# Attention stage of a two-layer kernel: key scores on 32 rows in pairs, projections and halves moved, a norm moved to ScalarE

## The chip, the cores and the metric

The program runs on one core of a Trainium2 chip. The metric is the device time of one execution in microseconds (us), lower is better. A run gives the median of several executions; one further execution was taken with the hardware profiler.

## The reference

Two layers over x of shape 4 x 512 x 128 (2048 tokens of 128 features). The change touches layer 0's attention and the layer norm and routing behind it. Cut to that:

```python
def _L0_attn_ref(x, WQ, WK, WV, WO):            # 16 heads of 8, causal
    Q, K, V = (heads(WQ), heads(WK), heads(WV))
    score = jnp.einsum('bhqd,bhkd->bhqk', Q, K) / jnp.sqrt(jnp.asarray(D_K, x.dtype))
    score = score + mask
    score = score - jnp.max(score, axis=-1, keepdims=True)
    score = jnp.exp(score)
    score = score / jnp.sum(score, axis=-1, keepdims=True)
    out = jnp.einsum('bhqk,bhkd->bhqd', score, V)
    out = out.transpose(0, 2, 1, 3).reshape(B, S, E)
    return out @ WO

x = L0_attn_x
x = x + _L0_attn_ref(_layernorm(x, axis=-1), WQ, WK, WV, WO)
x = x + _L0_ffn_ref(_layernorm(x, axis=-1), ...)   # 8 experts, top 2, fixed capacity
x = x + _L1_attn_ref(_layernorm(x, axis=-1), ...)  # gated linear attention + feed-forward
x = x + _L1_ffn_ref(_layernorm(x, axis=-1), ...)
```

## The kernel before

The program has three parts: layer 0's attention (up to about 214 us of the span), the eight experts, and layer 1. Only the first is changed.

**How attention is tiled.** There are 4 batches b of 512 tokens and 4 groups g of 4 heads, so 16 steps w = 4 b + g. Queries and keys are split into a rounded half and a rest and laid out as planes: a head takes 32 partitions (8 features in 3 or 4 planes, so that products of fp32r numbers come out near fp32). QS and QM are 128 x 512, four heads of 32 partitions. KP[:, s, j, i, :] is 128 x 128 for key tile j and head i, and holds numbers only on the 32 partitions of head i; the rest is zero. In a step these things are made:

- **row scores** of the step after (`row_scores`, line 1615): 10 units of 128 queries by 4 x 128 keys, 4 of them with a mask product (line 1618). VectorE takes the row maximum of each (`row_max`, line 1052) and frees the bank. They go round 3 PSUM banks (0 to 2), in the order that `_ring` gives, together with the two projections of the next batch.
- **turn_max** (line 1657): the maxima are transposed into bank 7, and `add_max` (line 1066, VectorE) adds them to QS, which gives QM.
- **key scores** (`key_scores`, line 1631): 12 units n, 4 heads for each of 3 chunks of key tiles: units 0 to 3 have one product of 512 columns, 4 to 7 one of 384, 8 to 11 two, of 256 and 128. They go round 3 more banks (3 to 5). Unit n waits for the exponential of unit n-3, which ScalarE makes (`exp_unit`, line 679). Units 10 and 11 are issued in the step after.
- **values** (`values`, line 1643): for key tile j, 4 heads, each with 32 output columns of the array and an fp32 moving operand (the trace gives their shape as 128*32, rows by columns of the array; all other matmuls are 128*128). They wait for `select` on GpSimd. values(w, 0) comes in step w, values 1 to 3 in step w+1.
- **turn_out** (line 1665) and `normalise` (VectorE) for the step before.

**Once a batch.** In the steps with g = 0, `project` (lines 1602, 1603) makes Q and K of the next batch, `round_halves` (line 669, ScalarE) rounds them to HL, `make_halves` (line 1042, VectorE) makes the rests and frees the two banks, and SyncE stores the planes to HBM and later loads them as QS and KP (`store_planes`, `pad`, lines 390 to 416). SyncE's KP of step G waits, from G = 3 on, for the key scores of step G-3. In the same steps `turn_heads` (line 1671) transposes the finished heads of the batch before, in g = 1 they are multiplied by WO (line 1677), VectorE adds them to X (line 1088) and makes the statistics of a layer norm (`stats_`, lines 957 to 963), GpSimd raises variances to -0.5 (`rsqrt`, line 521), and VectorE applies it (`norm`, line 969); in g = 2 the result is transposed (`turn_normed`) and gives the router's logits, in g = 3 the ranks.

**What sets the order.** Every engine's program is written out by hand in a loop over w; there is no scheduler. Semaphores tie the engines. Each engine runs its instructions in the order written.

Of the kernel before, what the change touches and what calls it, by code (L numbers as in the profile page):

```python
# [56 lines left out]
def _ring():  # L57

    at = {("q", 0): 0, ("k", 0): 1}
    for G in range(NW):  # L60
        for u in range(10):
            at[u, G] = len(at)
        if G % NG == 1 and G // NG + 1 < NB:
            at["q", G // NG + 1] = len(at)
            at["k", G // NG + 1] = len(at)
    return at
# [42 lines left out]
def build(nc, d):  # L109
    ctx = ExitStack()  # L110
    with ctx:
# [95 lines left out]
        with ExitStack() as attention:  # L207
# [15 lines left out]
            VR = early("VR", [P, NT, P])  # L223

# [85 lines left out]
        varA, rsA, xnA = sem("varA"), sem("rsA"), sem("xnA")  # L310
# [179 lines left out]
        def _(g):  # L490
# [58 lines left out]
            for w in range(NW):  # L549
# [4 lines left out]
                if at == 1 and before >= 0:  # L554
                    rsqrt(varA, rsA, before + 1)
# [86 lines left out]
        def _(act):  # L642
# [50 lines left out]

            def take_turn(what, b, dst):
# [42 lines left out]
            for w in range(NW):  # L737
# [4 lines left out]
                exp_unit(w, 0)  # L742
                if b and g == 2:
                    take_turn("turn2", b - 1, xn2T[:, :])
                exp_unit(w, 1)
# [7 lines left out]
                exp_unit(w, 5)  # L753
                exp_unit(w, 6)
                exp_unit(w, 7)
                if g == 0 and b + 1 < NB:
                    round_halves(b + 1)
                exp_unit(w, 8)
                if b and g == 0:
                    take_turn("turn", b - 1, OT[:, :])  # L760
                exp_unit(w, 9)
            exp_unit(NW - 1, 10)
# [171 lines left out]
        def _(v):  # L934
# [144 lines left out]
            def tail_of(b):  # L1079
# [9 lines left out]
                def stats_():  # L1089
                    v.wait_ge(tp_free, TURNS["wo", b] + 1)  # L1090
                    ln_stats(xt, link, varA)

                def norm():

                    v.wait_ge(scattered, b * 16 * TOPK * TB)
                    ln_apply(xt, lambda t: xn[:, t, :], rsA, b + 1, xnA)
# [55 lines left out]
                return add, stats_, norm, take_logits, choose, spread, ranks, place, count  # L1152
# [5 lines left out]
            for w in range(NW):  # L1158
                b, g = w // NG, w % NG
                rows_next = w + 1 < NW  # L1160
                if b and g == 0:
                    add, stats_, norm, take_logits, choose, spread, ranks, place, count = tail_of(b - 1)
                if rows_next:
# [404 lines left out]
        def _(pe):  # L1568
# [53 lines left out]
            def key_scores(w, n):  # L1622
# [555 lines left out]
```

## Time and profile before

| | us |
|---|---|
| median of 3 runs | 658.8 (657.65, 658.8, 662.22) |
| the profiled execution | 656.35, its span 654.6 |
| TensorE busy | 583.0 (89% of the span) |
| VectorE busy | 402.2 (61%) |
| ScalarE busy | 316.2 (48%) |
| GpSimd busy | 172.9 (26%) |
| mean granted TensorE clock | 0.965 |

Times in the trace are from the first instruction. PE is TensorE's matmuls, PEld its weight loads, DVE VectorE, ACT ScalarE, POOL GpSimd, SP SyncE. A matmul's duration in the trace reaches from its start to the end of its last output and overlaps that of its followers, so what TensorE spends on one is read from the distance between starts. An fp32 matmul shows as two records.

### The profile page before, as it was taken

The numbers are of one execution on the slowest core, as the hardware profiler recorded it, in microseconds if no ns is written. First come the engines' busy times: TensorE is split into PE (matmuls) and PEld (weight loads), VectorE is DVE, ScalarE is ACT, GpSimd is POOL, SyncE is SP. The second block draws the span as 40 slices with busy tenths as digits, with TensorE's granted clock in tenths as the row PEclk, the third lists the DMA queues.
The fourth block names the chain that finished last, engine by engine and source line by source line (L and its number), as shares of the span: only waits on it lengthen the run. The fifth ranks groups of instructions, "written<-read, shape, count | busy, mean of one in ns | idle before, by whom it ended". The sixth has DMA issues, their size and how long they took to land.

```text
span 654.6 us, 9264 instructions
## 1 busy us (share of the span) xinstructions
PE 583.0 (89%) x3347; PEld 433.0 (66%) x3347; DVE 402.2 (61%) x958; ACT 316.2 (48%) x543; POOL 172.9 (26%) x185
## 2 busy tenths in 40 slices
PE   8889989999998379999649698899999999998997
PEld 3556556556564258787536476688778878786866
DVE  6778788798884511432248986884669556762430
ACT  4756566556665204534216243752575255643351
POOL 6112122452543630000058623611300041001100
PEclk9999999999999579999969798999999999999999
DMA  4773242243110455834111100100000000000000
GB/s 130 223 247 110 77 130 65 82 145 97 55 44 2 137 167 167 263 90 118 41 32 32 30 4 2 34 0 1 1 17 2 1 0 18 1 0 1 18 1 17
DMA packets 44926, 42.51 MB, mean 65 GB/s; under 512 B 4176, under 2 KB 34384, under 8 KB 44880
## 3 DMA queue, kind: packets, MB, share of 16 engines
q1 hardware_dynamic: 42544, 37.44, 18.8%
q0 software_dynamic: 2048, 4.20, 2.2%
q8 instruction: 27, 0.44, 0.3%
q10 hardware_dynamic: 288, 0.28, 0.2%
q14 instruction: 19, 0.16, 0.1%
HBM read 25.12 MB, written 16.78 MB: 64 GB/s over the span
## 4 chain that ended last, share of the span: by engine, by line
PE 66%; DVE 10%; ACT 7%; issue 6%; DMA 5%; POOL 4%; SPq 2%; DVEq 0%; POOLq 0%; ACTq 0%
PE ps L1945 7%; PE ps L1615 6%; PE ps L1898 5%; PE ps L1631 5%; PE ps L1643 5%; PE ps L1967 5%; PE ps L1968 4%; PE ps L1889 4%; PE ps L2048 4%; PE ps L2044 4%; PE ps L2045 4%; PE ps L1971 4%; PE ps L1961 2%; DMA XS<-xs_dram 2%; PE ps L1618 2%
## 5 line engine op out<-in xcount | busy, mean ns | idle before, releaser
L679 ACT ACTIVATE PT<-ps 128x384 f32<-128x384 f32 (+1 forms) x192 | 93.5, 529 | 69.9 <-PE ps L1631 67.5
L1052 DVE TENSOR_REDUCE pm<-ps 128x4 f32<-128x512 f32 x160 | 102.3, 681 | 10.0 <-PE ps L1615 9.4
L1615 PE MATMUL ps<-KP,QS 128*128 128x512 f32 x160 | 71.7, 452 | 7.9 <-DVEq L1045 2.5
L546 POOL TENSOR_SCALAR_AFFINE_SELECT PT<-PT 128x512 f32<-128x512 f32 x64 | 39.9, 636 | 129.1 <-ACT PT L679 129.1
L1631 PE MATMUL ps<-QM,KP 128*128 128x512 f32 (+3 forms) x256 | 69.1, 331 | 1.5 <-DVE QM L1066 1.1
L1631 PEld LDWEIGHTS ps<-QM,KP 128*128 128x128 f32 x256 | 43.8, 189 | 22.8 <-issue 12.6
L796 ACT ACTIVATE HT<-ps,cols 128x640 f32<-128x640 f32 x32 | 25.4, 795 | 54.8 <-PE ps L1889 54.8
L1615 PEld LDWEIGHTS ps<-KP,QS 128*128 128x128 f32 x160 | 29.8, 188 | 27.5 <-DVE pm L1052 11.5
L1414 DVE TENSOR_TENSOR_SCAN zero<-decay,OG 128x512 f32<-128x512 f32 x32 | 44.8, 1400 | 1.1
L1643 PE MATMUL ps<-PT,V 128*32 128x128 f32 (+3 forms) x512 | 44.6, 442 | 0.0
L521 POOL TENSOR_TENSOR rstd<-veps,mhalf 128x4 f32<-128x4 f32 x11 | 12.7, 1157 | 110.7 <-DVE veps L963 110.5
L1898 PE MATMUL ps<-W,HT 128*128 128x128 f32 x320 | 37.8, 277 | 2.9 <-ACT HT L796 2.9
L1898 PEld LDWEIGHTS ps<-W,HT 128*128 128x128 f32 x320 | 36.3, 192 | 4.8 <-ACT HT L796 4.8
L853 ACT ACTIVATE hF<-ps,cols 128x512 f32<-128x512 f32 x16 | 11.0, 689 | 56.1 <-PE ps L2048 56.1
L1889 PE MATMUL ps<-XST,W 128*128 128x320 f32 x128 | 36.5, 438 | 1.1 <-DVE XST L1315 1.1
L1409 DVE SCALAR_TENSOR_TENSOR OG<-ps,cols,vs 128x512 f32<-128x512 f32 x32 | 23.9, 748 | 18.6 <-ACT vs L832 14.1
L836 ACT ACTIVATE gs<-ps,half_bg 128x512 f32<-128x512 f32 x32 | 22.0, 688 | 25.7 <-PE ps L1971 25.5
L611 POOL DMA_INDIRECT G<-ys_dram,posG x8 | 7.6, 950 | 93.0 <-DMA ys_dram<-zero 90.8
L832 ACT ACTIVATE vs<-ps,cols 128x512 f32<-128x512 f32 x32 | 22.0, 688 | 20.0 <-PE ps L1971 19.8
L582 POOL DMA_INDIRECT G<-ys_dram,posG x24 | 29.6, 1234 | 6.8 <-issue 6.8
L1889 PEld LDWEIGHTS ps<-XST,W 128*128 128x128 f32 x128 | 22.4, 190 | 12.1 <-ACT HT L796 4.5
L1945 PEld LDWEIGHTS ps<-lwo,oT 128*128 128x128 f32 x256 | 29.1, 192 | 0.2
(300 smaller groups left out, 1309.2 us busy)
## 6 DMA issues: line engine op xcount, KB each, us to landing
qk_dram<-HL SPq DMA_DIRECT2D x24, 256.0 KB, 3.5
W<-in_eW SPq DMA_DIRECT2D x16, 256.0 KB, 3.6
QS<-qk_dram SPq DMA_DIRECT2D x15, 256.0 KB
KP<-qk_dram SPq DMA_DIRECT2D x60, 64.0 KB, 2.4
xs_dram<-zero SPq DMA_DIRECT2D x4, 640.0 KB, 3.5
XS<-xs_dram SPq DMA_DIRECT2D x8, 320.0 KB, 5.0
ys_dram<-zero SPq DMA_DIRECT2D x8, 320.0 KB, 2.9
whole_h_w<-in_h_w SPq DMA_DIRECT2D x2, 1024.0 KB, 9.7
```

What stands on the lines that cost most here:

```text
L546: g.affine_select(out=diag, in_=diag, pattern=[[0, 4], [1, P]], compare_op=ALU.is_ge, fill=0.0, base=0, channel_multiplier=-1).then_inc(se ...
L582: g.indirect_dma_start(out=G[:, b % 2, i, :], out_offset=None, in_=ys_dram, in_offset=bass.IndirectOffsetOnAxis(ap=posG[:, c:c + 1], axis= ...
L679: act.activation(PT[:, i, a:z], bank[ROWB + n % KEYB][:, 0:z - a], ACT.Exp, scale=float(DK) ** -0.5).then_inc(exp_done, 1)
L1052: v.tensor_reduce(pm[:, t, k, :], bank[n % ROWB].rearrange("p (i n) -> p i n", n=P), AXX, ALU.max).then_inc(row_free[n % ROWB], 1)
L1414: v.tensor_tensor_scan(st, decay[:, f:f + 1].to_broadcast([P, SEQ]), kv, 0.0, ALU.mult, ALU.add).then_inc(st_done, 1)
L1615: mm = pe.matmul(to, QS[:, G % 2, t * P:(t + 1) * P], KP[:, G % 3, k, :, :].rearrange("p i n -> p (i n)"), start=True, stop=t != k)
L1631: mm = pe.matmul(bank[ROWB + n % KEYB][:, at:at + SEQ - j * P], KP[:, w % 3, j, i, :], QM[:, w % 2, j * P:SEQ], start=True, stop=True)
L1643: mm = pe.matmul(bank[6][32 * i:32 * i + 32, j * P:SEQ], V[:, j * H + g * 4 + i, :], PT[:, i, OFF[j]:OFF[j + 1]], start=(j == 0), stop=(j ...
L1889: mm = pe.matmul(ps[:, 2 * (f % 2) + a, 0:HALF], W1[:, s, f * P:(f + 1) * P], XST[:, s, a * HALF:(a + 1) * HALF], start=True, stop=True)
L1898: mm = pe.matmul(bank[4 + j // 4][:, (j % 4) * P:(j % 4 + 1) * P], HT[:, s, f, j * P:(j + 1) * P], W2[:, s, f, :], start=(f == 0), stop=(f ...
L1945: mm = pe.matmul(bank[5][:, t * P:(t + 1) * P], src[:, f, t * P:(t + 1) * P], w[:, f, :], start=(f == 0 and t == 0), stop=(f == n - 1), sk ...
L1967: pe.matmul(to, high[n][:, cs], halves_of[:, 0, :], start=True, stop=False)
```

## The change

Five edits, all in layer 0's attention.

1. `key_scores` takes rows 32 i to 32 i + 32 of KP and QM alone, where it took all 128 (with zeros on the others). The array is then used as a tile of 32 rows by 128 columns, at row 0, 32, 64 or 96. And TensorE's order puts the units in pairs: 0 with 1, 2 with 3, and so on to 10 with 11, where before most had a row score between them.
2. In steps g = 0 with a next batch, row_scores(w+2, 0) stands ahead of `project`, and both behind values(w, 0); before, the projections stood ahead of values(w, 0), and row_scores(w+2, 0) behind unit 8. `_ring` follows, and VectorE takes that row maximum ahead of the halves.
3. ScalarE rounds the halves ahead of exponentials 6 and 7, not behind them; it takes the transposed heads ahead of exponential 8.
4. The tail's layer norm is applied by ScalarE (four activations of 128 x 128, with scale and bias) behind exponential 9 of the step g = 1, not by VectorE. VectorE makes the negative means, GpSimd multiplies them by rstd.
5. Where a transposed tile is taken in g = 2, it stands behind exponential 1.

```diff
@@ _ring
         for u in range(10):
             at[u, G] = len(at)
-        if G % NG == 1 and G // NG + 1 < NB:
-            at["q", G // NG + 1] = len(at)
-            at["k", G // NG + 1] = len(at)
+            if u == 0 and G % NG == 2 and G // NG + 1 < NB:
+                at["q", G // NG + 1] = len(at)
+                at["k", G // NG + 1] = len(at)
@@ gpsimd
                 if at == 1 and before >= 0:
-                    rsqrt(varA, rsA, before + 1)
+                    g.wait_ge(varA, before + 1)
+                    g.tensor_tensor(rstd[:, :], veps[:, :], mhalf[:, 0:4], ALU.pow).then_inc(powA, 1)
+                    g.wait_ge(powA, before + 1)
+                    g.tensor_tensor(nmr[:, :], nm[:, :], rstd[:, :], ALU.mult).then_inc(rsA, 1)
@@ scalar
+            def norm(b):
+
+                act.wait_ge(scattered, b * 16 * TOPK * TB)
+                act.wait_ge(rsA, b + 1)
+                for t in range(TB):
+                    ins = act.activation(xn[:, t, :], X[:, b * TB + t, :], ACT.Identity, scale=rstd[:, t:t + 1],
+                                         bias=nmr[:, t:t + 1])
+                ins.then_inc(xnA, 1)
+
                 exp_unit(w, 0)
+                exp_unit(w, 1)
                 if b and g == 2:
                     take_turn("turn2", b - 1, xn2T[:, :])
-                exp_unit(w, 1)
...
                 exp_unit(w, 5)
+                if g == 0 and b + 1 < NB:
+                    round_halves(b + 1)
                 exp_unit(w, 6)
                 exp_unit(w, 7)
-                if g == 0 and b + 1 < NB:
-                    round_halves(b + 1)
-                exp_unit(w, 8)
                 if b and g == 0:
                     take_turn("turn", b - 1, OT[:, :])
+                exp_unit(w, 8)
                 exp_unit(w, 9)
+                if b and g == 1:
+                    norm(b - 1)
@@ vector
+                    v.tensor_scalar(nm[:, :], mv[:, :, 0], -1.0, None, ALU.mult)
+                    v.tensor_scalar(veps[:, :], mv[:, :, 1], EPS, None, ALU.add).then_inc(varA, 1)
...
-                if rows_next:
+                if rows_next and not (w and (w - 1) % NG == 0 and (w - 1) // NG + 1 < NB):
                     row_max(w + 1, 0)
...
                 if g == 0 and b + 1 < NB:
+                    row_max(w + 2, 0)
                     make_halves(b + 1)
-                if b and g == 1:
-                    norm()
@@ tensor, key_scores
-                    mm = pe.matmul(bank[ROWB + n % KEYB][:, at:at + SEQ - j * P], KP[:, w % 3, j, i, :],
-                                   QM[:, w % 2, j * P:SEQ], start=True, stop=True)
+                    mm = pe.matmul(bank[ROWB + n % KEYB][:, at:at + SEQ - j * P], KP[32 * i:32 * i + 32, w % 3, j, i, :],
+                                   QM[32 * i:32 * i + 32, w % 2, j * P:SEQ], start=True, stop=True)
@@ tensor, the loop over w
                 if rows_next:
                     row_scores(w + 1, 9)
-                if g == 0 and b + 1 < NB:
+                values(w, 0)
+                if early:
+                    row_scores(w + 2, 0)
                     project(b + 1)
-                values(w, 0)
                 key_scores(w, 6)
                 key_scores(w, 7)
                 if b and g == 0:
                     turn_heads(b - 1)
                 if b and g == 2:
                     logits(b - 1)
+                if w + 2 < NW and not early:
+                    row_scores(w + 2, 0)
                 key_scores(w, 8)
-                if w + 2 < NW:
-                    row_scores(w + 2, 0)
                 key_scores(w, 9)
```

The changed lines move all line numbers: row scores are L1634 after, masks L1637, key scores L1650, values L1662, turn_max L1676, the projections L1621 and L1622, exponentials L684.

TensorE's instructions in the middle of step 1, before, from row_scores(2, 3) to unit 3 (L1615 row scores, L1618 mask, L1631 key scores):

```order
L1615 MATMUL ps<-KP,QS 128x512 [waits row_free0]
L1631 MATMUL ps<-QM,KP 128x512 [waits exp_done,tp_free]
L1615 MATMUL ps<-KP,QS 128x512 [waits row_free1]
L1618 MATMUL ps<-mask,identr 128x512
L1631 MATMUL ps<-QM,KP 128x512 [waits exp_done]
L1615 MATMUL ps<-KP,QS 128x512 [waits row_free2]
L1618 MATMUL ps<-mask,identr 128x512
L1631 MATMUL ps<-QM,KP 128x512 [waits exp_done]
L1615 MATMUL ps<-KP,QS 128x512 [waits row_free0]
L1631 MATMUL ps<-QM,KP 128x512 [waits exp_done]
```

The same place after:

```order
L1634 MATMUL ps<-KP,QS 128x512 [waits row_free0]
L1650 MATMUL ps<-QM,KP 128x512 [waits exp_done,tp_free]
L1650 MATMUL ps<-QM,KP 128x512 [waits exp_done]
L1634 MATMUL ps<-KP,QS 128x512 [waits row_free1]
L1637 MATMUL ps<-mask,identr 128x512
L1634 MATMUL ps<-KP,QS 128x512 [waits row_free2]
L1637 MATMUL ps<-mask,identr 128x512
L1650 MATMUL ps<-QM,KP 128x512 [waits exp_done] x2
L1634 MATMUL ps<-KP,QS 128x512 [waits row_free0]
```

Units 0 and 1, and 2 and 3, which were four single products with row scores between, stand as two pairs; the number of products is the same.

TensorE at the end of step 0, before, from the projections to row_scores(2, 1) (L1602 and L1603 projections, L1643 values):

```order
L1602 MATMUL ps<-xnT,wq 128x512 [waits row_free1]
L1603 MATMUL ps<-xnT,wk 128x512 [waits row_free2]
L1643 MATMUL ps<-PT,V 32x512 [waits v_ready,sel_done]
L1643 MATMUL ps<-PT,V 32x512 x3
L1631 MATMUL ps<-QM,KP 128x384 [waits exp_done] x2
L1631 MATMUL ps<-QM,KP 128x256 [waits exp_done]
L1631 MATMUL ps<-QM,KP 128x128
L1615 MATMUL ps<-KP,QS 128x512 [waits kp_in2,qs_in0,row_free0]
L1631 MATMUL ps<-QM,KP 128x256 [waits exp_done]
L1631 MATMUL ps<-QM,KP 128x128
L1615 MATMUL ps<-KP,QS 128x512 [waits row_free1]
```

And after:

```order
L1662 MATMUL ps<-PT,V 32x512 [waits v_ready,sel_done]
L1662 MATMUL ps<-PT,V 32x512 x3
L1634 MATMUL ps<-KP,QS 128x512 [waits kp_in2,qs_in0,row_free1]
L1621 MATMUL ps<-xnT,wq 128x512 [waits row_free2]
L1622 MATMUL ps<-xnT,wk 128x512 [waits row_free0]
L1650 MATMUL ps<-QM,KP 128x384 [waits exp_done] x2
L1650 MATMUL ps<-QM,KP 128x256 [waits exp_done]
L1650 MATMUL ps<-QM,KP 128x128
L1650 MATMUL ps<-QM,KP 128x256 [waits exp_done]
L1650 MATMUL ps<-QM,KP 128x128
L1634 MATMUL ps<-KP,QS 128x512 [waits row_free1]
```

The row score that waits for kp_in2 and qs_in0 (KP and QS of step 2, loads from HBM) stood behind the projections, the values and units 6 to 8; it stands right behind the values, ahead of the projections.

ScalarE in step 5 (b = 1, g = 1), before, from the exponentials of units 8 to 11 to step 6's taking of xn2T:

```order
L679 ACTIVATE PT<-ps 128x384 [waits ts_full,pv_done]
L679 ACTIVATE PT<-ps 128x384 [waits ts_full] x3
L679 ACTIVATE PT<-ps 128x512 [waits ts_full,pv_done]
L697 ACTIVATE xn2T<-ps 128x512 [waits tp_full]
L679 ACTIVATE PT<-ps 128x512 [waits ts_full] x3
```

And after:

```order
L684 ACTIVATE PT<-ps 128x384 [waits ts_full,pv_done]
L684 ACTIVATE PT<-ps 128x384 [waits ts_full]
L704 ACTIVATE xn<-X,nmr,rstd 128x128 [waits rsA,scattered]
L704 ACTIVATE xn<-X,nmr,rstd 128x128 x3
L684 ACTIVATE PT<-ps 128x384 [waits ts_full] x2
L684 ACTIVATE PT<-ps 128x512 [waits ts_full,pv_done]
L684 ACTIVATE PT<-ps 128x512 [waits ts_full]
L711 ACTIVATE xn2T<-ps 128x512 [waits tp_full]
```

The four activations of the norm stand between exponentials 9 and 10.

## Rows read from the trace of the kernel before

**Rows 1.** The profile page: busy us of each engine, share of the span, instructions.

```profile
PE 583.0 (89%) x3347; PEld 433.0 (66%) x3347; DVE 402.2 (61%) x958; ACT 316.2 (48%) x543; POOL 172.9 (26%) x185
```

**Rows 2.** Windows, steps 2, 4, 5: length; PE, PEld, DVE, ACT, POOL busy; clock, DMA share, GB/s.

```profile
51.24:61.24 10.00, 10.00 (x73) 6.38 (x71) 8.20 (x16) 6.35 (x13) 2.49 (x4) 1.00 0.35 120
...
71.24:84.86 13.62, 12.64 (x81) 7.66 (x80) 9.58 (x18) 8.24 (x18) 2.49 (x4) 1.00 0.20 59
84.86:97.71 12.85, 11.96 (x85) 7.55 (x88) 11.29 (x32) 7.09 (x15) 3.50 (x5) 1.00 0.46 144
```

**Rows 3.** PE timeline of step 2: start us, duration us, line, operation, array shape, count.

```profile
54.75 0.39 PE L1631 MATMUL ps<-QM,KP 128*128 128x512 f32 x1
55.06 0.86 PE L1643 MATMUL ps<-PT,V 128*32 128x256 f32 x16
55.85 0.50 PE L1615 MATMUL ps<-KP,QS 128*128 128x512 f32 x1
56.19 0.34 PE L1631 MATMUL ps<-QM,KP 128*128 128x384 f32 x1
56.38 0.40 PE L1615 MATMUL ps<-KP,QS 128*128 128x512 f32 x1
...
59.81 0.45 PE L1631 MATMUL ps<-QM,KP 128*128 128x256 f32 x2
60.09 0.44 PE L1615 MATMUL ps<-KP,QS 128*128 128x512 f32 x1
60.38 0.39 PE L1618 MATMUL ps<-mask,identr 128*128 128x512 f32 x1
60.61 0.60 PE L1657 MATMUL ps<-const,MX 128*128 128x128 f32 x4
```

**Rows 4.** PEld timeline there: the two weight loads behind the values.

```profile
55.85 0.19 PEld L1615 LDWEIGHTS ps<-KP,QS 128*128 128x128 f32 x1 [0.20 <-issue]
55.96 0.19 PEld L1631 LDWEIGHTS ps<-QM,KP 128*128 128x128 f32 x1
```

**Rows 5.** PE groups by form: values of 128 columns.

```profile
L1643 PE MATMUL ps<-PT,V 128*32 128x128 f32 x128 | 6.5, 273 | 0.0
```

**Rows 6.** PE timeline of step 0, around the wait for KP.

```profile
35.89 1.07 PE L1643 MATMUL ps<-PT,V 128*32 128x512 f32 x8
...
39.60 0.47 PE L1615 MATMUL ps<-KP,QS 128*128 128x512 f32 x1 [1.92 <-DMA KP<-qk_dram]
...
40.61 0.60 PE L1657 MATMUL ps<-const,MX 128*128 128x128 f32 x4
```

**Rows 7.** PE timeline of step 4: projections, values, the stall behind them.

```profile
77.70 1.02 PE L1602 MATMUL ps<-xnT,wq 128*128 128x512 f32 x2
...
79.71 1.07 PE L1643 MATMUL ps<-PT,V 128*32 128x512 f32 x8
80.71 0.61 PE L1631 MATMUL ps<-QM,KP 128*128 128x384 f32 x2
...
83.38 0.50 PE L1615 MATMUL ps<-KP,QS 128*128 128x512 f32 x1 [0.98 <-DVEq L1045]
...
83.97 0.66 PE L1657 MATMUL ps<-const,MX 128*128 128x128 f32 x4
```

**Rows 8.** PE timeline of step 5: the stall ahead of row scores.

```profile
92.02 0.50 PE L1615 MATMUL ps<-KP,QS 128*128 128x512 f32 x1 [0.89 <-DVE pm L1052]
```

**Rows 9.** PE timeline of step 6: row scores behind the values, then key scores.

```profile
98.31 0.51 PE L1615 MATMUL ps<-KP,QS 128*128 128x512 f32 x1
98.66 0.40 PE L1631 MATMUL ps<-QM,KP 128*128 128x512 f32 x1
```

**Rows 10.** DVE timeline of step 5: the norm.

```profile
95.70 1.48 DVE L969 TENSOR_SCALAR xn<-X,mv,rstd 128x128 f32<-128x128 f32 x4
```

**Rows 11.** ACT timeline of step 4: exponentials 6 and 7, halves.

```profile
81.19 0.87 ACT L679 ACTIVATE PT<-ps 128x384 f32<-128x384 f32 x2 [3.32 <-PE ps L1631]
81.94 1.09 ACT L669 ACTIVATE HL<-ps 128x512 fp32r<-128x512 f32 x2
```

More of the change, by code:

```diff
@@ L223, in build @@
             VR = early("VR", [P, NT, P])
+            nm = early("nm", [P, 4])
+            nmr = early("nmr", [P, 4])
         wide = ("Wv", "Wk", "Wg", "Wq")
@@ L309, in build @@
         mx_done, qm_done = sem("mx_done"), sem("qm_done")
-        varA, rsA, xnA = sem("varA"), sem("rsA"), sem("xnA")
+        varA, powA, rsA, xnA = sem("varA"), sem("powA"), sem("rsA"), sem("xnA")
         og_done, lT = sem("og_done"), sem("lT")
@@ L1090, in stats_ @@
                     v.wait_ge(tp_free, TURNS["wo", b] + 1)
[L1091 to L1096, printed above, removed]
+                    v.sem_inc(v_paced, 1)
+                    for t in range(TB):
+                        ins = v.bn_stats(stats[:, t, :], xt(t))
+                    link(ins)
+                    v.sem_inc(v_paced, 1)
+                    for t in range(TB):
+                        ins = v.bn_aggr(mv[:, t, :], stats[:, t, :])
+                    link(ins)
+                    v.tensor_scalar(nm[:, :], mv[:, :, 0], -1.0, None, ALU.mult)
+                    v.tensor_scalar(veps[:, :], mv[:, :, 1], EPS, None, ALU.add).then_inc(varA, 1)
                 def take_logits():
@@ L1150, in count @@
                     assert link.k == NLT, link.k
-                return add, stats_, norm, take_logits, choose, spread, ranks, place, count
+                return add, stats_, take_logits, choose, spread, ranks, place, count
             make_halves(0)
@@ L1161, in _ @@
                 if b and g == 0:
-                    add, stats_, norm, take_logits, choose, spread, ranks, place, count = tail_of(b - 1)
-                if rows_next:
+                    add, stats_, take_logits, choose, spread, ranks, place, count = tail_of(b - 1)
+                if rows_next and not (w and (w - 1) % NG == 0 and (w - 1) // NG + 1 < NB):
                     row_max(w + 1, 0)
@@ L1740, in _ @@
                 rows_next = w + 1 < NW
+                early = g == 0 and b + 1 < NB
                 turn_max(w)
@@ L1743, in _ @@
                     key_scores(w - 1, 10)
+                    key_scores(w - 1, 11)
                 if rows_next:
@@ L1746, in _ @@
                 if w:
-                    key_scores(w - 1, 11)
                     values(w - 1, 1)
@@ L1751, in _ @@
                 key_scores(w, 0)
+                key_scores(w, 1)
                 if b and g == 1:
@@ L1759, in _ @@
                     row_scores(w + 1, 4)
-                key_scores(w, 1)
-                if rows_next:
                     row_scores(w + 1, 5)
                 key_scores(w, 2)
+                key_scores(w, 3)
                 if rows_next:
                     row_scores(w + 1, 6)
-                key_scores(w, 3)
                 if w:
@@ L1772, in _ @@
                 key_scores(w, 4)
+                key_scores(w, 5)
                 if rows_next:
                     row_scores(w + 1, 8)
-                key_scores(w, 5)
                 if w:
```

## The prediction

> **What bounds the kernel now.** I read the page first, then windows by step, then TensorE's timeline of one step beside its weight loads. The page shows TensorE busy 89% of the span, and the next engine, VectorE, 61% [rows 1]. A busy share does not say what a stage waits for, so I looked at steps. Step 2, where nothing of the once-a-batch work runs, takes 10.00 us, with TensorE busy all of it, VectorE 8.20, ScalarE 6.35 and the clock at 1.00, its upper level of 2.4 GHz [rows 2]. The reader is to see that it is TensorE's own instruction stream that lasts 10 us there: a microsecond added to the stream or taken from it moves the end. Step 4 (projections) takes 13.62 and step 5 (norm) 12.85, and there TensorE idles for about a microsecond each [rows 2, 7, 8].
>
> **What a change of the array's shape costs.** The one question that decides the case is what a pair of 32-row products costs, and the trace has none. It has the nearest relation: values use the array as 128*32, everything else as 128*128. Between products of one shape, starts are 0.23 us apart for 512 columns (60.38 to 60.61), also where fp32r is followed by fp32, 0.19 for 384 (56.19 to 56.38) and 0.28 for a unit of 256 + 128 (59.81 to 60.09) [rows 3]. Into the values it is 0.31 (54.75 to 55.06), so 0.08 more [rows 3]. Out of them: the block's records end at 55.92, the last of them 0.27 long, so it started at 55.65 [rows 3, 5]; the next weight load starts at 55.85, and behind it the second weight load follows after 0.11 [rows 4]. A product of 128 columns needs that same 0.11 before its follower, so 0.09 is lost; and since no weights were loaded ahead, the first load of 0.11 lies open: the next start is at 56.19, 0.34 behind and not 0.23 [rows 3]. A block of another shape thus costs 0.08 to enter and 0.20 to leave. One of 128-column weights also has its own first load of 0.11 open (the values' weights have 32 columns). Together 0.40 for a pair of key scores.
>
> The Trainium skill, TensorEngine Tiling, section Tiling Modes, states that a change of tiling mode drains TensorE; the trace agrees, for columns. The Trainium skill's TensorEngine Tiling, section Theoretical Speedup, gives up to four times for a contraction of 32 and doesn't count switches there; no row here shows a row tile. By the first rule the sum is the forecast's, by the second alone it is that of the first rival.
>
> **Edit 1, pairs.** The two products of a pair write different banks and use different rows, and I take them to overlap fully, as the values' four heads do (8 records of 512 columns, two of each, in 1.07 us [rows 6]). Then, for each pair: 512 columns, before 2 x 0.23 = 0.46, after 0.23 + 0.40 = 0.63, +0.17. 384 columns, before 0.38, after 0.19 + 0.40 = 0.59, +0.21. 256 + 128, before 0.56, after 0.28 + 0.40 = 0.68, +0.12. A step has two pairs of each: +1.00. The pair 6, 7 stands right behind the values, where the exit of 0.20 is paid already: +0.80. Unit 9 waits for ScalarE's exponential 6 today, so a little of it is hidden: I take 0.75 a step, and for the 14 steps 1 to 14 **+10.5 us**. Step 15 has no row scores between its units; I take nothing for it. Bounds: nothing for a switch (the spacing between equal shapes), and 0.11 more a pair if the second weight load doesn't go beside the first.
>
> **Edit 2 in step 0.** The row score of step 2 waits for KP until 39.60; TensorE has by then done projections, values and units 6 to 8, and still idles 1.92 us; turn_max follows 1.01 later, at 40.61 [rows 6]. The load doesn't come earlier, for SyncE's order is unchanged. Now the projections stand behind this wait. From 39.60: the row score 0.34, projections 2.0 (77.70 to 79.71 [rows 7]), then ScalarE's second half, about 0.1 + 0.55, exponential 6 0.49 (two take 0.87, two halves 1.09 [rows 11]), unit 9 0.28, leaving the shape 0.2, row score and mask 0.46: turn_max at about 44.0. **+3.4 us**. TensorE would idle over 4 us at one go.
>
> **Edits 2 and 3 in steps 4 and 8.** There KP has landed. Before, from 77.70 to turn_max at 83.97 it is 6.27, with a stall of 0.98 until VectorE has freed the bank of the query projection [rows 7]. After: values 1.1, row score 0.34, projections 2.0, then ScalarE's chain of 0.65 for the half, 0.87 for exponentials 6 and 7 and about 0.6 for the heads (a half, of the same 512 columns, takes 0.55 [rows 11]), which frees bank 7 for turn_max: 5.6. **-0.65 each, -1.3.** What is late next: exponential 8, and with it unit 11, by some tenths, covered by turn_max.
>
> **Edit 4.** VectorE loses 1.48 us in steps 5, 9 and 13 [rows 10]. But behind that norm TensorE waits for nothing: the key score at 98.66 is 0.35 behind its row score at 98.31, which is the open weight load behind the values and no more [rows 9]. So it is worth nothing where TensorE is the bound. ScalarE takes it, four activations, at most as long as four exponentials (1.9 us), beside 5.8 of idle time (7.09 of 12.85 busy [rows 2]); if that cover were gone, units 1 and 2 of the next step would wait for exponentials 10 and 11. GpSimd's extra product stands ahead of its select 1, which has microseconds to spare. The stall in step 5 is that of 0.89 [rows 8] (9 and 13 are taken alike), behind VectorE's add and statistics, which stay, with one small operation more; TensorE comes some 0.4 later to it: **-0.25 each, -0.75**. Edit 5 moves a copy by one exponential: nothing.
>
> **Sum.** 10.5 + 3.4 - 1.3 - 0.75 = +11.9. The profiled execution took 656.35, so 668.2; it lies 2.45 under the median of the runs and 1.3 under their lowest, so I say **669**.
>
> **Rivals.**
> - *Row tiles need no drain, and the pairs gain.* Each pair then costs one product: -0.23 twice, -0.19 once and -0.28 once a step; units 6 to 9 stay tied to ScalarE: -0.93, for 14 steps -13. Step 0 keeps its 3.4, steps 4 and 8 their 1.3; in the norm steps VectorE holds some 0.4 back. About -10: **647**, faster. For it: in a row tile each head's rows and bank are its own. Against it: the values switch columns only, and pay. It decides from a price for a whole block below 0.2. 0.28.
> - *Neither overlap nor drain.* Steps stay at 10.0, leaving 3.4 - 1.3 - 0.75: **660**. For it: fp32r may not share the array. 0.15.
> - *More than the columns' price*: the second load isn't beside the first (0.11 x 6 x 14 = 9 more), or the clock falls to 1.2 GHz behind step 0's long wait: **673 to 678**. 0.12.
> - *As forecast*: 0.45, own range 662 to 674.
>
> **Numbers.** Faster or slower by 1%, 6.6 us, is about what a measurement of this kernel can tell. The forecast case and the dearer one give slower 0.50, with 0.07 of the former inside 1%; the rival without overlap adds 0.15: same 0.22; faster 0.28. The range has to reach into the gaining rival: 646 to 675.
>
> **What would show it.** Step 2's window: 10.7 to 10.9 us if right, 9.1 if the drain is missing, 10.0 without both. Starts of key scores: two within hundredths of each other, then 0.09 and 0.11 open at the next row score. In step 0 a row score with over 4 us of idle time ahead, 1.92 today [rows 6], and no stall on L1045's successor in steps 4 and 8. The stalls ahead of row scores in the norm steps stay. It is wrong if a 128*128 product starts 0.23 behind a pair.

## The result, and the profile after

| | before | after |
|---|---|---|
| median of the runs, us | 658.2 (655.7 to 662.2, 4 runs) | 679.1 (670.3 to 680.6, 4 runs) |
| ratio | | 1.0267, 95% interval 1.0152 to 1.0383 |
| profiled execution, and its span | 656.35, 654.6 | 679.37, 677.6 |
| mean granted TensorE clock | 0.965 | 0.942 |

The changed kernel is slower, by 21 us where 669 and so about 11 were forecast. It lies above the range's upper end of 675. Three of the four executions took 679 to 681 us; the fourth took 670.3, inside the range, and wasn't traced; the trace below is of one of the three. Of two kernels below (e2_step0, e8_pairs_alone) the profiled execution lay above those that their ratio compares, at a lower mean clock (0.929 against 0.953 to 0.961, and 0.925 against 0.941 and 0.949); what is said of their time goes by the ratio.

From the page of after, to be read beside [rows 1]: busy time of the engines, and the granted clock in 40 slices of 16.9 us, in tenths of 2.4 GHz.

```profile
PE 606.1 (89%) x3347; PEld 427.2 (63%) x3347; DVE 399.5 (59%) x949; ACT 317.9 (47%) x555; POOL 173.2 (26%) x188
PEclk9966999999999658999987989999999999999999
```

The clock line of before (slices of 16.4 us):

```profile
PEclk9999999999999579999969798999999999999999
```

TensorE is busy 23 us longer, as much as the span grew, and the other engines are where they were. The 6 in the third and fourth slice is new: a stretch at a lower clock in steps 0 and 1. The windows of steps 0 to 2, 4 and 5 of after, from turn_max to turn_max (columns: busy us of PE, PEld, DVE, ACT, POOL, then the clock and the DMA share):

```profile
28.62:46.81 18.19, 12.79 (x44) 6.12 (x43) 9.20 (x17) 6.84 (x13) 1.27 (x2) 0.77 0.61 187
46.81:64.49 17.68, 17.68 (x72) 8.24 (x70) 8.51 (x16) 5.99 (x13) 2.40 (x4) 0.56 0.34 111
64.49:75.32 10.83, 10.83 (x71) 5.58 (x70) 8.23 (x16) 6.25 (x14) 2.49 (x5) 1.00 0.31 110
86.15:99.26 13.11, 13.11 (x79) 6.57 (x78) 9.61 (x18) 7.75 (x17) 2.49 (x5) 1.00 0.21 58
99.26:112.16 12.90, 11.86 (x80) 6.48 (x79) 9.96 (x27) 6.64 (x15) 3.69 (x7) 1.00 0.49 149
```

Step 2 is what was forecast: 10.83 against 10.00 [rows 2], at full clock. Step 4 is 0.25 shorter than before and step 5 is 0.51 longer. Step 1 does the work of step 2 and takes 6.85 longer, with TensorE busy in all of it and a clock of 0.56. One stretch at half the clock runs through step 0's end and most of step 1; two windows of after show it, before and during:

```profile
28.62:38.60 9.98, 6.35 (x30) 2.89 (x28) 7.12 (x14) 3.90 (x7) 0.64 (x1) 1.00 0.73 212
38.60:62.40 23.80, 22.03 (x74) 10.15 (x74) 9.72 (x18) 7.45 (x15) 2.49 (x4) 0.50 0.41 136
```

The clock fell at 38.60, 1.2 us ahead of the end of a wait. It stands in TensorE's timeline of after (start, us, engine, line and operation, idle time ahead and what ended it) and is the one that the second edit made longer, 1.92 us before [rows 6]:

```profile
39.80 0.76 PE L1634 MATMUL ps<-KP,QS 128*128 128x512 f32 x1 [4.42 <-DMA KP<-qk_dram]
40.36 1.91 PE L1621 MATMUL ps<-xnT,wq 128*128 128x512 f32 x2
```

The pairs themselves, first by shape in step 2 of after (busy us and mean ns of one), then in the timeline of step 3, matmuls and weight loads. They answer to [rows 3, 4]:

```profile
L1650 PE MATMUL ps<-QM,KP 32*128 32x512 f32 x4 | 1.0, 496 | 0.0
```

```profile
77.45 0.49 PE L1634 MATMUL ps<-KP,QS 128*128 128x512 f32 x1
77.87 0.50 PE L1650 MATMUL ps<-QM,KP 32*128 32x512 f32 x2
78.30 0.50 PE L1634 MATMUL ps<-KP,QS 128*128 128x512 f32 x1
78.64 0.40 PE L1637 MATMUL ps<-mask,identr 128*128 128x512 f32 x1
...
79.11 0.39 PE L1637 MATMUL ps<-mask,identr 128*128 128x512 f32 x1
79.42 0.50 PE L1650 MATMUL ps<-QM,KP 32*128 32x512 f32 x2
```

```profile
78.30 0.19 PEld L1634 LDWEIGHTS ps<-KP,QS 128*128 128x128 f32 x1 [0.24 <-issue]
78.41 0.19 PEld L1637 LDWEIGHTS ps<-mask,identr 128*128 128x128 f32 x1
```

Four products of 0.496 us are busy 1.0 us in all, so the two of a pair lie wholly over each other. From a row score to the pair it is 0.42, from the pair to the next row score 0.43, where products of one shape stand 0.23 apart. Behind the exit the weights of the mask product are loaded 0.11 after the row score's, and it starts 0.34 behind it and not 0.23: the first product behind a block makes its follower 0.11 late. The row score at 77.45 is such a first product, behind the values, so 0.11 of its 0.42 belongs to the values' exit. The mask product at 79.11 is not, and there the pair starts 0.31 behind. A pair thus costs about 0.1 to enter, 0.20 to leave and 0.11 at the follower of the next product: 0.4 in all.

The steps of the kernels that follow, turn_max to turn_max, us:

| step | before | after | e1_awake | e3_full | e4_full_step0 |
|---|---|---|---|---|---|
| 0 | 12.19 | 18.19 | 15.07 | 16.57 | 12.19 |
| 1 | 10.00 | 17.68 | 10.85 | 10.09 | 10.08 |
| 2, 3 | 10.00, 10.00 | 10.83, 10.83 | 10.83, 10.83 | 10.04, 10.09 | 10.08, 10.08 |
| 4, 8 | 13.36, 14.12 | 13.11, 13.27 | 13.11, 13.43 | 12.38, 12.98 | 12.42, 13.00 |
| 5, 9, 13 | 12.39, 12.09, 12.10 | 12.90, 12.59, 12.58 | 12.90, 12.59, 12.57 | 12.54, 12.22, 12.16 | 12.54, 12.24, 12.15 |
| 7, 11 | 10.72, 10.72 | 11.20, 11.20 | 11.20, 11.20 | 10.73, 10.73 | 10.72, 10.72 |
| 0 to 14 | 171.6 | 190.4 | 180.7 | 174.2 | 169.9 |
| from step 15 to the end | 454.6 | 458.6 | 454.6 | 456.7 | 455.8 |

### The profile page after: what moved, and what is told of

The parts are those of the page before. It is cut to its first block, busy times and chain, and to the rows that moved or that the text cites. A ratio compares the mean times of both kernels' runs of the same rounds, so it can differ in the third digit from the quotient of the medians.

```text
span 677.6 us, 9270 instructions
## 1 busy us (share of the span) xinstructions
PE 606.1 (89%) x3347; PEld 427.2 (63%) x3347; DVE 399.5 (59%) x949; ACT 317.9 (47%) x555; POOL 173.2 (26%) x188
## 4 chain that ended last, share of the span: by engine, by line
PE 71%; DVE 7%; ACT 6%; issue 5%; DMA 4%; POOL 3%; SPq 2%; DVEq 0%; POOLq 0%; ACTq 0%
PE ps L1634 8%; PE ps L1965 6%; PE ps L1662 6%; PE ps L1650 5%; PE ps L1918 5%; PE ps L1987 5%; PE ps L1909 4%; PE ps L2068 4%; PE ps L2064 4%; PE ps L1988 4%; PE ps L2065 4%; PE ps L1991 4%; PE ps L1981 2%; DMA XS<-xs_dram 2%; PE ps L1637 2%
## 5 line engine op out<-in xcount | busy, mean ns | idle before, releaser
L684 ACT ACTIVATE PT<-ps 128x384 f32<-128x384 f32 (+1 forms) x192 | 90.1, 525 | 72.9 <-PE ps L1650 72.8
L1634 PE MATMUL ps<-KP,QS 128*128 128x512 f32 x160 | 79.3, 502 | 8.6 <-DMA KP<-qk_dram 4.4
L1634 PEld LDWEIGHTS ps<-KP,QS 128*128 128x128 f32 x160 | 30.7, 194 | 39.5 <-issue 25.0
L1650 PE MATMUL ps<-QM,KP 32*128 32x256 f32 (+3 forms) x256 | 49.6, 402 | 2.2 <-ACT PT L684 1.1
L1650 PEld LDWEIGHTS ps<-QM,KP 32*128 32x128 f32 x256 | 25.6, 192 | 39.0 <-issue 29.6
L1662 PE MATMUL ps<-PT,V 128*32 128x128 f32 (+3 forms) x512 | 49.0, 479 | 0.0
L1909 PE MATMUL ps<-XST,W 128*128 128x320 f32 x128 | 38.2, 454 | 1.1 <-DVE XST L1334 1.1
L523 POOL TENSOR_TENSOR rstd<-veps,mhalf 128x4 f32<-128x4 f32 x8 | 9.6, 1204 | 110.1 <-DVE veps L979 110.1
```

The source lines that it names most:

```text
L684: act.activation(PT[:, i, a:z], bank[ROWB + n % KEYB][:, 0:z - a], ACT.Exp, scale=float(DK) ** -0.5).then_inc(exp_done, 1)
L1634: mm = pe.matmul(to, QS[:, G % 2, t * P:(t + 1) * P], KP[:, G % 3, k, :, :].rearrange("p i n -> p (i n)"), start=True, stop=t != k)
L1662: mm = pe.matmul(bank[6][32 * i:32 * i + 32, j * P:SEQ], V[:, j * H + g * 4 + i, :], PT[:, i, OFF[j]:OFF[j + 1]], start=(j == 0), stop=(j ...
L1909: mm = pe.matmul(ps[:, 2 * (f % 2) + a, 0:HALF], W1[:, s, f * P:(f + 1) * P], XST[:, s, a * HALF:(a + 1) * HALF], start=True, stop=True)
```

## The experiments

The theory after reading the trace: the changes of shape cost about 0.8 us a step; step 0's order costs some 3 us; and what is beyond the forecast is the clock, which falls behind step 0's wait and then stays at 1.2 GHz while key scores use 32 rows. The rivals: the clock's fall is an accident of the wait alone, or the gaps at changes of shape hold it down.

### e1_awake: no idle time in step 0's wait

```diff
                 values(w, 0)
+                if w == 0:
+                    for _ in range(17):
+                        pe.matmul(tiles(tp_bank), identr[:, :],
+                                  identr[:, :].rearrange("p (a n) -> p a n", a=1).to_broadcast([P, 4, P]),
+                                  start=True, stop=True)
                 if early:
                     row_scores(w + 2, 0)
```

> The changed kernel with 17 products of 512 columns, whose result nobody uses, on TensorE between values(0, 0) and the row score of step 2, where the changed kernel idles 4.42 us. Theory (clock): in the changed kernel the clock is at 1.2 GHz from 38.6 to 62.4 us because of that wait; with TensorE busy it stays at 2.4 GHz, steps 0 and 1 (between starts of turn_max) go from 18.19 and 17.68 to about 15.6 and 10.8, the time from 679 to about 669 to 670, and no execution is like the others' 679. Rival (the wait for KP and contention alone are the loss, or the clock falls whatever TensorE does there): steps 0 and 1 stay at 18 and 17.7, time 679.

Measured 667.6 (665.4 to 671.9, 4 runs), ratio 1.0197 (1.0156 to 1.0237). Steps 0 and 1 of e1_awake:

```profile
28.36:43.42 15.06, 13.93 (x60) 7.88 (x59) 9.21 (x17) 6.52 (x13) 1.18 (x2) 1.00 0.67 188
43.42:54.27 10.85, 10.85 (x71) 5.58 (x70) 8.23 (x16) 6.16 (x14) 2.51 (x5) 1.00 0.73 235
```

The same program with the same wait, its idle time filled with products that nobody uses, is 11.5 us faster. No window of steps 0 to 14 falls below 1.00, and step 1 is a step of 10.85 like its neighbours. So 6.8 us of step 1 and 3.1 of step 0 are the clock. What is left, 9.1 us in steps 0 to 14, is what the forecast's 11.9 was about. The time is 2 us under the 669 to 670 expected.

### e2_step0: step 0 in the order of before

```diff
-                early = g == 0 and b + 1 < NB
+                early = w and g == 0 and b + 1 < NB
...
+                if w == 0:
+                    project(1)
                 values(w, 0)
```

> The changed kernel with step 0 in the order of before (projections, values, units 6 and 7, then the row score that waits for KP). Theory: the wait shrinks to 1 to 2 us, the clock stays up, step 0 is back at 12.2 to 12.8, step 1 at 10.8; time about 665 to 666 (679 less 3.4 less 9.4). Rival (step 0's order is innocent, the pairs draw the clock down): still 675 or more.

Measured ratio 1.0154 (1.0129 to 1.0180), 666.5 by the median. In the profiled execution the wait in step 0 is short, but the clock falls behind it all the same, and stays down for two steps. Its windows of steps 0 to 2, and the wait:

```profile
27.81:39.77 11.96, 9.87 (x43) 4.66 (x42) 9.11 (x17) 6.51 (x13) 1.28 (x2) 1.00 0.82 256
39.77:58.51 18.74, 18.74 (x72) 8.73 (x71) 8.51 (x16) 6.63 (x15) 2.50 (x4) 0.50 0.36 124
58.51:76.03 17.52, 17.52 (x71) 8.23 (x70) 8.51 (x16) 6.00 (x14) 2.41 (x4) 0.56 0.21 68
```

```profile
38.40 0.47 PE L1638 MATMUL ps<-KP,QS 128*128 128x512 f32 x1 [1.68 <-DMA KP<-qk_dram]
```

Its executions lie at 666 (three) or at 681 (two, of which this is one). None of those at 666 was traced; that the clock fell less in them is read from their mean clock. So the long wait is not needed for the fall; a wait of 1.68 is enough in some executions. In the kernel before, with 1.92 us of idle time at this place, the profiled execution shows no fall here, and the ten executions of e4_full_step0 below, which is this kernel with 128 rows, all took 655 to 659. So with key scores on 32 rows a shorter wait is enough.

### e3_full and e4_full_step0: key scores on 128 rows again

```diff
-KP[32 * i:32 * i + 32, w % 3, j, i, :], QM[32 * i:32 * i + 32, w % 2, j * P:SEQ]
+KP[:, w % 3, j, i, :],                  QM[:, w % 2, j * P:SEQ]
```

e3_full is the changed kernel with that alone; e4_full_step0 has step 0's old order too, and so is the remaining edits.

> The changed kernel with key scores on all 128 rows again, in the same order of pairs. Theory (array shape): step 2 falls from 10.83 to 10.0 us, and the 14 steps give back some 0.8 each, about 10 us; the long wait of step 0 and its slow clock stay: 667 to 670. A row score behind a pair starts 0.23 behind it, not 0.43. Rival (the order of the pairs itself costs, through banks and exponentials): step 2 stays at 10.8.

> Key scores on 128 rows, and step 0 in the order of before: what is left is the order of pairs, the early row score in steps 4 and 8, the halves ahead of exponentials, the norm on ScalarE. Theory: steps 2, 3 at 10.0, steps 4 and 8 1 us shorter than before's 13.36 and 14.12, the rest as before: 655 to 657 against 658.2. Rival (the moved norm and halves cost): 660 or more.

e3_full measured 659.7, ratio 1.0046 (1.0026 to 1.0067); e4_full_step0 656.3, ratio 1.0002 (0.9985 to 1.0020). In e3_full the wait is the same as in after, and the stretch at half clock is another:

```profile
38.63 0.47 PE L1634 MATMUL ps<-KP,QS 128*128 128x512 f32 x1 [4.52 <-DMA KP<-qk_dram]
```

```profile
39.40:42.80 3.40, 3.40 (x8) 1.84 (x6) 1.14 (x3) 1.25 (x3) 0.00 (x0) 0.50 0.13 26
42.80:44.00 1.20, 1.02 (x7) 0.74 (x7) 0.67 (x1) 1.20 (x4) 0.42 (x1) 1.00 0.98 321
54.07:64.11 10.04, 10.04 (x71) 6.39 (x70) 8.13 (x17) 6.15 (x14) 2.49 (x5) 1.00 0.35 119
```

3.4 us against 23.8. That is why e3_full lies under the 667 to 670 expected, which had the long stretch stay. The price of the rows at full clock is e1_awake less e3_full: 0.74 to 0.79 in each of steps 1 to 3, 8.0 us in steps 1 to 14. Step 0's order costs 4.4 (16.57 against 12.19), with its 3.4 us at 1.2 GHz in it. The other edits shorten steps 4 and 8 by 0.94 and 1.12, step 12 by 0.39, and lengthen the norm steps by 0.05 to 0.15; steps 0 to 14 are 1.7 shorter in all, what follows is 1.2 longer, and the time is the same.

### e5_32_alone: 32 rows without pairs

The kernel before, with the edit of e3_full the other way round, and no other.

> The kernel before with one edit: key scores take 32 rows, and nothing is reordered, so most units stand alone between row scores. If each change of the array's shape costs about 0.4 us (what the changed kernel's steps show for a pair), the seven units that now stand alone cost 0.4 each and units 3 and 11, which stand beside values, 0.2 to 0.4 more: step 2 takes 13 to 13.5 us instead of 10.00, and the whole some 45 us more, about 700. The rival is that the rows cost nothing and the 0.83 us a step came from standing in pairs (two units waiting on ScalarE at one place): then step 2 takes 10.0 to 10.2 and the time is 657 to 660.

Measured 725.9 (720.5 and 731.3), ratio 1.1054 (1.0953 to 1.1155). Its step 2 ran at 1.2 GHz in part, so step 3, 12.77 at a clock of 1.00, is the one to read; and a lone unit in TensorE's timeline:

```profile
84.65:97.42 12.77, 12.62 (x71) 6.18 (x70) 8.33 (x16) 6.58 (x14) 2.49 (x5) 1.00 0.27 92
```

```profile
87.13 0.49 PE L1615 MATMUL ps<-KP,QS 128*128 128x512 f32 x1
87.55 0.50 PE L1631 MATMUL ps<-QM,KP 32*128 32x512 f32 x1
87.98 0.50 PE L1615 MATMUL ps<-KP,QS 128*128 128x512 f32 x1
```

In at 0.42, out at 0.43, as with a pair (here too the row score ahead stands right behind the values): a block costs the same whether one unit stands in it or two. Seven lone units by 0.40 are 2.8, and the step is 2.78 longer than before; I had added some tenths for the units beside values, and nothing is left for them. The rival (the pair's place, and not the rows) is out. The time is 26 us above the 700 expected, and the rest of the 69 us is again the clock: step 1 takes 20.5 us. Its trace shows two long stretches at 1.2 GHz, and what stands ahead of the second:

```profile
45.10:82.70 37.60, 37.60 (x125) 15.97 (x118) 15.28 (x30) 11.10 (x21) 4.34 (x7) 0.50 0.27 89
...
129.18:144.10 14.92, 14.92 (x88) 8.18 (x86) 9.58 (x33) 7.47 (x15) 2.58 (x5) 1.00 0.13 36
144.10:185.10 41.00, 41.00 (x137) 18.78 (x137) 18.51 (x45) 12.15 (x23) 8.43 (x11) 0.50 0.15 45
```

TensorE is busy for 14.9 us without idle time, and the clock falls at 144.10 all the same. So with lone units on 32 rows no wait is needed for a fall. Whether the rows or the gaps bring it on here was not tried apart: this kernel has more gaps, 2.8 us a step, than e12_gaps below with 1.7, whose clock held on full rows. And since nine of a step's twelve units stand alone here, two products running side by side are not needed for a stretch of 37.6 or 41.0 us either.

### e7_full_steps01 and e12_gaps: what holds the clock down

e7_full_steps01 is the changed kernel with all rows in the key scores of steps 0 and 1. e12_gaps has all rows everywhere, and a tiny product of another shape ahead of five pairs a step:

```diff
+                if n % 2 == 0 and n != 6:
+                    pe.matmul(bank[ROWB + n % KEYB][0:32, 0:32], identr[:, 0:32].bitcast(F32),
+                              identr[:, 0:32].bitcast(F32), start=True, stop=True)
```

> The changed kernel, with the key scores of steps 0 and 1 on all 128 rows and those of steps 2 to 15 on 32. Theory: products on 32 rows keep TensorE at 1.2 GHz once it has fallen behind the wait for KP in step 0. Then the clock is back within 3 to 5 us of the end of that wait, as with full rows everywhere, step 0 takes 16.6, step 1 about 10.1, the others stay as in the changed kernel, and the time is about 670. Rival: which rows are used has nothing to do with it, and the execution with full rows everywhere had its clock back early for another cause; then 1.2 GHz lasts over 20 us again and the time is 677 to 680.

> The changed kernel with key scores on all 128 rows, and ahead of five of the six pairs of a step an unused product of 32 columns by 32 (in a corner of the bank that the pair overwrites), which uses the array as 128*32. So the stream has as many changes of shape as the changed kernel's, and about as much idle time of the array, but every product uses all 128 rows. The wait of 4.4 us in step 0 is as there. Both theories give a step 2 of 12 to 13 us. Theory one, the rows decide the clock: it is back at 2.4 GHz 3 to 8 us after the wait, as with full rows; step 1 takes 12 to 14 us. Theory two, the gaps at changes of shape decide: 1.2 GHz lasts over 20 us, and step 1 takes 18 us or more.

e7_full_steps01 measured 671.2 (670.7 to 671.6, 4 runs), ratio 1.0219 (1.0194 to 1.0245). Its stretch at 1.2 GHz, the rest up to step 2, step 2 and step 3:

```profile
37.30:44.10 6.80, 5.33 (x10) 3.00 (x11) 1.98 (x3) 1.82 (x4) 0.00 (x0) 0.50 0.35 116
44.10:54.84 10.74, 10.74 (x74) 6.94 (x75) 8.19 (x17) 6.76 (x16) 2.89 (x5) 1.00 0.71 234
54.84:65.59 10.75, 10.75 (x71) 5.71 (x70) 8.26 (x17) 6.30 (x14) 2.64 (x5) 1.00 0.33 111
65.59:76.42 10.83, 10.83 (x72) 5.58 (x71) 8.24 (x16) 6.25 (x14) 2.49 (x5) 1.00 0.32 109
```

The clock is back 5.4 us behind the end of the wait (38.66), a little over the 3 to 5 expected. Eight microseconds come back by giving two of sixteen steps their rows back, and the steps on 32 rows that follow run at full clock: in pairs and without a long wait the rows don't make it fall there (alone they did, in e5_32_alone); behind a fall they keep it from rising again. e12_gaps took 679.7 (678.5 to 679.7, 3 runs), ratio 1.0330 (1.0285 to 1.0376), for it does more; what it was made for is its stretch at half clock and its step 2:

```profile
38.60:42.00 3.40, 2.99 (x4) 1.51 (x5) 0.69 (x1) 0.40 (x1) 0.00 (x0) 0.50 0.14 59
56.24:67.95 11.71, 11.71 (x81) 6.93 (x80) 8.23 (x16) 6.26 (x15) 2.49 (x5) 1.00 0.30 102
```

With 11.71 a step there are more gaps than in the changed kernel's 10.83, and the clock is back after 3.4 us. The gaps are out; of the two theories it is the rows. Step 1 took 11.7, a little under the 12 to 14 expected, since a block of 32 columns costs 0.33.

### e8_pairs_alone and e10_norm_alone: single edits on the kernel before

e8_pairs_alone is edit 1 alone; e10_norm_alone is edit 4 alone.

> The kernel before with the first edit alone: key scores on 32 rows and in pairs, step 0, the halves and the norm as before. Theory: 0.83 us a step from 1 to 14 for six blocks of another shape, nothing for clock in the fastest executions: 657 + 11.6 = 668.5, or 667 if the other edits, which came out at nothing in sum, are worth nothing here either (with them and with step 0 in the old order it was 666.5). Rival: part of the 0.83 is hidden where the once-a-batch steps wait for other engines, and those waits take it in: 662 to 665.

> The kernel before with the fourth edit alone: the tail's norm on ScalarE. The prediction gave it 0.25 us in each of steps 5, 9 and 13; the changed kernel with full rows had 12.54, 12.24 and 12.15 there, against 12.39, 12.09 and 12.10. Theory now: it is worth nothing or slightly less, steps 5, 9, 13 take 12.4 to 12.6, 12.1 to 12.3, 12.1 to 12.2, and the time is 656.5 to 657.5. Rival: the norm did help and the pairs' order took it back; then these steps take 12.1, 11.8, 11.9 and the time is 656 or less.

e8_pairs_alone: ratio 1.0301 (1.0254 to 1.0348), 677, eight to ten more than the theory's 667 to 668.5, and twelve or more above the rival's; its four executions took 675, 678, 687 and 688. Its step at full clock is the known one (10.84), but in the profiled execution 1.2 GHz holds twice, in steps 1 and 2 and again in step 5, right behind the wait that edits 2 and 3 take away:

```profile
101.29 0.50 PE L1615 MATMUL ps<-KP,QS 128*128 128x512 f32 x1 [1.04 <-DVEq L1045]
```

```profile
101.87:118.14 16.27, 16.27 (x79) 8.84 (x79) 11.01 (x29) 6.32 (x14) 3.37 (x5) 0.69 0.43 128
76.97:87.81 10.84, 10.84 (x72) 5.57 (x71) 8.23 (x16) 6.24 (x14) 2.49 (x5) 1.00 0.31 109
```

That the one wait brought the fall on is read from their order; it wasn't tried apart. e10_norm_alone: 657.2 (10 runs), ratio 1.0006 (0.9983 to 1.0030). Its steps 5 and 9:

```profile
83.05:95.49 12.44, 11.47 (x79) 7.26 (x79) 10.75 (x29) 6.59 (x14) 3.46 (x6) 1.00 0.56 167
131.47:143.63 12.16, 11.48 (x79) 7.24 (x79) 10.69 (x29) 6.60 (x14) 6.40 (x9) 1.00 0.67 191
```

12.44 against 12.39, 12.16 against 12.09: the norm on ScalarE gives nothing, as then expected.

### e6_keys, e11_before_keys and e9_full_step0_keys: the wait removed at its source

SyncE issues the four transfers of KP for step 2 ahead of the pads of batches 2 and 3 and the biases (those of batch 1 stay ahead), in the changed kernel, in the kernel before, and in e4_full_step0. In pad(2), KP goes ahead of QS:

```diff
             pad(1)
-            for b in range(1, NB):
+            store_pads(1)
+            pad(2)
+            for b in range(2, NB):
                 store_pads(b)
```

> The changed kernel, with SyncE's four transfers of KP for step 2 issued ahead of the padding of batches 1 to 3 and of the row biases instead of behind them. Theory: the 4.4 us wait in step 0 is one for KP's place in SyncE's queue. With KP there, step 0 is 12 to 13.5 us long, the clock doesn't fall to 1.2 GHz, step 1 takes 10.8, and the time is 664 to 666, under the 667.6 of the version that kept TensorE busy through the wait. Rival: KP comes no earlier, since it waits for its zeros or for HBM; step 0 stays at 16 to 18 and the time at 677 to 680; or the later padding delays a later step by as much as is gained.

> The kernel before with the early load of KP for step 2 alone. Theory: the wait of 1.92 us ahead of the row score in step 0 goes, 655 to 655.5, as with the other edits beside it. Rival: 1.9 us before KP something else ends as late (ScalarE's exponential 6, the halves), and less than 1 us is gained: 656 to 657.

> The changed kernel with key scores on all 128 rows, step 0 in the order of before, and KP of step 2 loaded ahead of the padding of the later batches. Without the early load it measured the same as the kernel before (656.3). Theory: the early load takes the wait of 1.9 us out of step 0, which then takes 10.3 to 10.9 instead of 12.19, with nothing given back later: 654.5 to 655.5. Rival: what comes later in the queue (pads of batches 1 to 3, biases) arrives late and gives it back, or the end of attention takes it in: 656 to 657.

e6_keys: 665.0 (660.4 to 669.0, 4 runs), ratio 1.0119 (1.0055 to 1.0182), so the place in the queue was the wait; step 0 takes 10.91, where 12 to 13.5 were expected. Its steps 0 and 1:

```profile
28.52:39.43 10.91, 9.81 (x43) 4.78 (x42) 9.11 (x17) 6.52 (x13) 1.18 (x2) 1.00 0.68 198
39.43:50.27 10.84, 10.84 (x72) 5.58 (x71) 8.24 (x16) 6.16 (x14) 2.50 (x5) 1.00 0.80 296
```

In the kernel before the same load gives nothing (656.7, ratio 0.9997, 0.9976 to 1.0019): the rival held. The row score's place is then released by VectorE's halves, which edits 2 and 3 have out of the way:

```profile
39.31 0.50 PE L1626 MATMUL ps<-KP,QS 128*128 128x512 f32 x1 [1.21 <-DVEq L1056]
```

e9_full_step0_keys is faster than both kernels, half a percent under before: 654.3 (12 runs), ratio 0.9946 (0.9925 to 0.9968). Its profiled execution was the slowest of the twelve. In it step 0 takes 10.30 for 12.19; 0.9 is given back in step 1, to KP of step 3:

```profile
47.56 0.47 PE L1649 MATMUL ps<-KP,QS 128*128 128x512 f32 x1 [0.90 <-DMA KP<-qk_dram]
```

## Why the prediction was wrong, step by step

**The step that failed** is the sum's term for step 0, "+3.4 us". It wrote down over 4 us of idle time at one go, but priced it as a delay only, and put the clock behind it at nothing, without a reason. The fall stood only in the rival "more than the columns' price", where it says "or the clock falls to 1.2 GHz behind step 0's long wait", with a chance of 0.12 shared with another cause and a ceiling of 678. It cost 9.7 us in steps 0 to 14 (190.4 less e1_awake's 180.7), all but some tenths of it in steps 0 and 1, and more than any term but the pairs'. That it lasts 23.8 us and not 3.4 comes from the 32 rows, and no row of the kernel before shows such a product at either clock. Of the span's 23.0 us, step 0's order is 2.9, steps 1 to 14 at full clock are 6.2 (e1_awake less before), the clock 9.7, and 4.0 lie behind the attention; the last 0.2 lie ahead of step 0. With the clock up, the forecast's +11.9 came out at 9.1, too high by 2.8, and its 669 at e1_awake's 667.6.

**A block of another shape, 0.40.** The sum of its parts was right, the split was not. The forecast had 0.08 to enter, 0.11 for the block's own weights, and 0.20 to leave with the follower's 0.11 in it. Measured are about 0.1 to enter, weights and all (79.11 to 79.42, where products of one shape stand 0.23 apart), 0.20 ahead of the next product, and 0.11 more ahead of that one's follower. That two errors of 0.1 cancel is luck. The Trainium skill, TensorEngine Tiling, section Tiling Modes, states that a change of mode drains TensorE; the trace agrees for rows too (the 0.20 lost behind a pair). The pairs overlap fully, as taken. Step 2 came out at 10.83, inside 10.7 to 10.9.

**Pairs, +10.5.** Too much: 8.0 for steps 1 to 14, against 10.5, or 9.75 with what was taken off in the norm steps. By e1_awake less e3_full the 0.75 a step holds in steps 1 to 4, 6 and 10 (0.70 to 0.79). In steps 7, 8, 11, 12 and 14 it is 0.41 to 0.59 and in the norm steps 5, 9 and 13 0.36 to 0.41, where TensorE also waits for VectorE, once a step. The term multiplied the cleanest step's price by all steps; why the other steps pay less was not followed up.

**Step 0's order, +3.4.** As a delay, right in mechanism and idle time (4.42), and near in size: 4.4 in e3_full with its 3.4 us at half clock, 2.9 in e1_awake without.

**Steps 4 and 8, -0.65 each.** Right in sign, too small: -0.94 and -1.12 in e4_full_step0. TensorE no longer waits on the successor of L1045 there. In TensorE's timeline of step 4 of after nothing stands ahead of the row score that closes it:

```profile
98.14 0.62 PE L1650 MATMUL ps<-QM,KP 32*128 32x256 f32 x4
98.69 0.50 PE L1634 MATMUL ps<-KP,QS 128*128 128x512 f32 x1
```

**Norm steps, -0.25 each.** Right with the pairs (+0.50 forecast, +0.51, +0.50 and +0.48 measured), and near in its parts: some 0.4 of the pairs' 0.75 was to be taken in, and the price of the rows there is 0.36 to 0.41, so 0.34 to 0.39 were; the other edits add 0.15, 0.13 and 0.06 (e3_full less before), and edit 4 alone 0.05 to 0.07. Edit 4 itself gave nothing, as the forecast's own argument had it. Which wait took the pairs' price in is not shown. The stall that was to do it did not shrink; it comes later and is 1.01 in step 5 of after, against 0.89 before [rows 8]:

```profile
107.87 0.50 PE L1634 MATMUL ps<-KP,QS 128*128 128x512 f32 x1 [1.01 <-DVE pm L1068]
```

**The gaining rival** is out: no step is shorter for its pairs. **Behind the attention** 4.0 us were added in after, with 1.2 GHz for 31 us at its end and in the experts' first part instead of 20.5; e1_awake, which ends the attention with the same products, added nothing there, but its profiled execution was its fastest. e9_full_step0_keys, faster than before, has 458.7 us there, and e7_full_steps01 460.2. So one trace each doesn't tell how much of the 4.0 belongs to the change; this is left open. The window of after:

```profile
222.90:267.20 44.30, 28.63 (x141) 17.80 (x141) 14.13 (x82) 10.13 (x22) 19.53 (x22) 0.65 0.37 113
```

## What to carry to other kernels

Take a forecast of idle time on TensorE for two prices: the delay, and the clock behind it; ask what products follow the wait, since here they decided how long 1.2 GHz lasted. A small contraction put on a tile of 32 rows saves nothing unless the products that overlap in a block save more than the 0.4 us that the block costs; here a pair saves one product, about 0.2, and pays 0.4. A stream with many lone products on 32 rows can lose the clock without any wait, as in e5_32_alone. And a wait for a transfer is best removed in the queue that issues it: the move of four transfers gave 14 us to the changed kernel and nothing to the kernel before, where another engine was as late.

## What the runs showed of the hardware that I had not expected

- After a fall TensorE stayed at 1.2 GHz for 23.8 us (after) and for some 34 us (e2_step0) where key scores used 32 rows, though it was busy in all of the steps behind the wait (17.68 of 17.68 us in step 1 of after, 18.74 and 17.52 in steps 1 and 2 of e2_step0); with 128 rows it was back in 3.4 us (e3_full, e12_gaps) and 6.8 us (e7_full_steps01). The Trainium skill, TensorE: Matmul & The Clock Gate, section What's actually happening, says that activity releases the throttle; by the trace a busy engine alone does not, and the measurement decides. Why rows count is not shown here. That two products run side by side is not needed for it: in e5_32_alone nine of twelve units stand alone, and 1.2 GHz lasted 37.6 and 41.0 us.
- With lone units on 32 rows the clock fell in the midst of work: in e5_32_alone at 144.10, behind 14.9 us in which TensorE was busy without idle time.
- The same wait doesn't always bring a fall: with 1.68 us of idle time and 32 rows, executions lay at 666 or at 681.
- A block on a row tile of 32 costs about 0.1 us to enter and 0.20 to leave, and the follower of the first full product behind it starts 0.11 late; a unit alone pays the same as a pair.
